# Reordering the first step of a fused Perceiver layer: weight loads, key products, key norms and the threefold query row

## The reference

```python
x = x + cross_attention(layernorm(x), ctx)   # x 1x128x512, ctx 1x12544x512, 16 heads of 32
x = x + self_attention(layernorm(x))         # 16 heads of 128, FP4 codes times scales as weights
x = x + moe(layernorm(x))                    # 32 experts of 256, 4 chosen per row, and a shared one

# cross_attention:
q     = rms_norm(x @ q_w.T + q_b) * norm_q_w
k_img = rms_norm(ctx[:257] @ k_img_w.T + k_img_b) * norm_k_img_w
v_img = ctx[:257] @ v_img_w.T + v_img_b
k, v  = the same of ctx[257:], with k_w, v_w, ... of their own
out   = (attention(q, k_img, v_img) + attention(q, k, v)) @ o_w.T + o_b
```

## Time and profile before

| | us |
|---|---|
| median of three executions | 1211.16 |
| lowest, highest | 1208.44, 1211.66 |
| span of the profiled execution | 1210.0 |
| TensorE, VectorE, ScalarE, GpSimd busy | 1172.7, 979.3, 853.0, 763.8 |

### The profile page before, as it was taken

One profiled execution on the slowest core, in us unless ns is written; L12 is line 12 of the kernel. 1 busy time (PEld: TensorE's weight loads), 2 busy tenths in 40 slices (PEclk: granted clock), 3 DMA queues, 4 the chain that ended last, 5 costly groups with the idle time before them and its releaser, 6 DMA issues.

```text
span 1210.0 us, 26425 instructions
## 1 busy us (share of the span) xinstructions
PE 1172.7 (97%) x8794; PEld 940.5 (78%) x8794; DVE 979.3 (81%) x1657; ACT 853.0 (70%) x1845; POOL 763.8 (63%) x1064
## 2 busy tenths in 40 slices
PE   6999999999999999999999999999999779899998
PEld 4768888888888888888888888888887558588886
DVE  4768888878888888888888887888877779499997
ACT  5567777777767777777777777677777757378885
POOL 7987888888888878788887888888873100000000
PEclk9999999999999999999999999999999989999999
DMA  7135686665776667756668666686653899469990
GB/s 253 41 97 154 164 218 168 172 171 151 212 177 176 166 168 186 207 155 175 171 168 215 168 175 163 154 218 171 175 135 97 257 394 397 190 253 366 360 365 21
DMA packets 132400, 236.74 MB, mean 196 GB/s; under 512 B 18086, under 2 KB 45222, under 8 KB 131884
## 3 DMA queue, kind: packets, MB, share of 16 engines
q1 hardware_dynamic: 132268, 235.06, 66.4%
HBM read 140.87 MB, written 17.04 MB: 130 GB/s over the span
## 4 chain that ended last, share of the span: by engine, by line
PE 89%; POOL 5%; DVE 2%; issue 1%; ACT 1%; DMA 1%; SPq 0%; POOLq 0%; DVEq 0%; ACTq 0%
PE ps L1500 36%; PE ps L1363 18%; PE ps L1526 9%; PE ps L1570 8%; PE ps L1694 3%; PE ps L1697 3%; PE ps L1700 3%; PE ps L1715 1%; PE ps L1723 1%; PE ps L1719 1%; PE ps L1671 1%; PE ps L1610 1%; PE ps L1614 1%; PE ps L1607 1%; POOL cx_blocks L613 1%
## 5 line engine op out<-in xcount | busy, mean ns | idle before, releaser
L1500 PE MATMUL ps<-w_text,cx_blocks 128*128 128x512 f32 x1974 | 536.7, 397 | 1.3 <-ACT v_first L803 0.7
L1500 PEld LDWEIGHTS ps<-w_text,cx_blocks 128*128 128x128 f32 x1974 | 366.4, 189 | 65.8 <-issue 2.7
L846 ACT ACTIVATE p<-ps,small 128x512 f32<-128x512 f32 (+2 forms) x400 | 271.1, 678 | 203.1 <-DVE small L1167 199.7
L1165 DVE TENSOR_REDUCE small<-ps 128x1 f32<-128x512 f32 (+2 forms) x400 | 270.6, 677 | 110.2 <-PE ps L1526 109.9
L1363 PE MATMUL ps<-ident,p 128*128 128x128 f32 x1584 | 239.8, 273 | 8.8 <-DVE pt L1158 7.0
L1363 PEld LDWEIGHTS ps<-ident,p 128*128 128x128 f32 x1584 | 193.9, 140 | 63.9 <-issue 12.4
L1526 PE MATMUL ps<-k_stack,q_stack 96*128 96x512 f32 (+1 forms) x400 | 191.9, 480 | 1.2 <-ACT p L846 1.2
L828 ACT ACTIVATE pt<-ps 128x512 f32<-128x512 f32 (+1 forms) x250 | 147.6, 591 | 12.3 <-PE ps L1363 8.0
L615 POOL TENSOR_TENSOR cx_blocks<-cx_sum,cx_blocks 128x256 fp32r<-128x256 f32 x188 | 139.3, 741 | 14.8
L613 POOL TENSOR_TENSOR cx_blocks<-cx_sum,small 128x256 fp32r<-128x256 f32 x188 | 118.2, 629 | 44.8 <-PE ps L1500 37.0
L1167 DVE TENSOR_TENSOR small<-small 128x1 f32<-128x1 f32 x400 | 132.4, 331 | 13.7
(11 more groups left out here) (252 smaller groups left out, 1935.2 us busy)
## 6 DMA issues: line engine op xcount, KB each, us to landing
expert<-experts SPq DMA_DIRECT2D x34, 1536.0 KB, 8.7
k_stack<-kt_hi SPq DMA_DIRECT2D x384, 128.0 KB, 2.5
cx<-ctx_t SPq DMA_DIRECT2D x48, 512.0 KB, 4.4
k_stack<-kt_lo SPq DMA_DIRECT2D x192, 128.0 KB, 2.5
codes<-codes SPq DMA_DIRECT2D x64, 256.0 KB, 4.5
code_scale<-code_scales SPq DMA_DIRECT2D x256, 64.0 KB, 4.0
scaled<-codes SPq DMA_DIRECT2D x64, 256.0 KB, 4.4
weight_q<-scaled SPq DMA_DIRECT2D x1, 4096.0 KB, 15.6
```

The lines of the kernel that those rows point to most:

```text
L846: eng.activation(pb[:, lo:hi], score_bank(s, h)[:, lo:hi], exp, bias=nm[1 - par][:, h:h + 1], accum_out=ls[1 - par][:, h:h + 1]).then_inc( ...
L1165: eng.tensor_reduce(ngm[:, h:h + 1], score_bank(s, h)[:, lo:hi], AX.X, ALU.max, negate=True).then_inc(e_gm, 1)
L1500: last = eng.matmul(ps_a[(p + i + 1) % 2][:, :], blk[:, i, a, c * P:(c + 1) * P], w_t[:, i, w, c * D:(c + 1) * D], start=(i in FRESH and c ...
```

## The change

It touches the first step alone:

- SyncE issues the image key weights ahead of the two further context tiles and of wq.
- TensorE does `product(0, 0)` and `product(0, 1)` ahead of the query's product and the last three spread rows.
- VectorE stores the first two key tiles ahead of the query; the image value split comes behind the query's bias. The threefold repeat leaves VectorE: it makes a plain 128x512 product into `q_sq`, and ScalarE repeats it into `q_thrice`, as it did before for the text part's query.
- GpSimd has the norms of key tiles 0 and 1 ahead of the query's norm; between that and `first_pair`'s low part nothing is left.
- ScalarE squares two key tiles ahead of the query, squares the third ahead of storing the first transposes, and then repeats the query.

```diff
@@ sync
             eng.dma_start(img_cx[:, :, 0:P], cxt[:, :, 0:P]).then_inc(e_cx0, 16)
+            load_weight(0)
             eng.dma_start(img_cx[:, :, P:IT * P], cxt[:, :, P:IT * P]).then_inc(e_cx, 16)
             eng.dma_start(wq[:, :, :], wview(t["q_wt"])).then_inc(e_wq, 16)
-            load_weight(0)
             load_weight(1)
@@ gpsimd, image()
                 eng.tensor_tensor(pair_hi[:, :, :], keys, ones.broadcast_to((P, DC, 2 * P)), ALU.mult).then_inc(e_ahi, 1)
+                key_norm(0, 0, 1)
+                key_norm(0, 1, 1)
                 eng.wait_ge(e_qsq, 1)
                 eng.tensor_scalar(r_t, q_ss, RMS_EPS, float(HD), ALU.add, ALU.mult).then_inc(e_pool, 1)
                 n_pool[0] += 1
                 eng.wait_ge(e_pool, n_pool[0])
                 eng.tensor_tensor(q_r, r_t, minus_half, ALU.pow).then_inc(e_rs, 1)
 
-                key_norm(0, 0, 1)
                 eng.wait_ge(e_ahi, 1)
                 eng.tensor_tensor(pair_lo[:, :, :], keys, pair_hi[:, :, :].bitcast(F32), ALU.subtract).then_inc(e_ab, NPOS)
                 eng.wait_ge(e_w[2], 16)
                 eng.wait_ge(e_w[3], 16)
                 eng.tensor_tensor(t1[:, :, :], b12, b11, ALU.subtract).then_inc(e_tt, 1)
-                key_norm(0, 1, 1)
@@ scalar
+            def repeat_queries(i, of):
+
+                eng.wait_ge(e_qh, i + 1)
+                eng.activation(q_thrice[i][:, :, :].rearrange("p h (r d) -> p h r d", r=NST),
+                               of[:, :].rearrange("p (h d) -> p h d", h=NH).unsqueeze(2).broadcast_to((P, NH, NST, HD)),
+                               copy).then_inc(e_q3, 1)
...
                 split_weight(1)
+                square_keys(0, *IMAGE_TILES[0])
+                eng.wait_ge(e_sq, 1)
+                square_keys(0, *IMAGE_TILES[1])
                 eng.wait_ge(e_qb, 1)
                 eng.activation(q_sq[:, :], qf[:, :], square, scale=D ** -0.5, accum_out=q_ss).then_inc(e_qsq, 1)
-                square_keys(0, *IMAGE_TILES[0])
                 for i in range(3, NROW):
                     store_row(i)
                 scale_keys(0, *IMAGE_TILES[0])
                 split_weight(2)
-                square_keys(0, *IMAGE_TILES[1])
-                keys_high(0, *IMAGE_TILES[0])
                 eng.wait_ge(e_sq, 2)
                 square_keys(0, *IMAGE_TILES[2])
+                keys_high(0, *IMAGE_TILES[0])
+                repeat_queries(0, q_sq)
@@ vector, image()
-                eng.wait_ge(e_rowc, 1)
+                eng.wait_ge(e_rowc, 2)
+                keys(0)
+                keys(1)
                 eng.wait_ge(e_qp, 1)
                 eng.tensor_tensor(qf[:, :], ps_s[0][:, :], q_rows[:, 0, :], ALU.add).then_inc(e_qb, 1)
-                eng.wait_ge(e_rowc, 2)
-                keys(0)
                 split_weight(1)
                 eng.wait_ge(e_rowc, NROW)
                 eng.wait_ge(e_rs, 2)
                 chain(eng.scalar_tensor_tensor(qn[:, :], qf[:, :], q_r, q_rows[:, 1, :], ALU.mult, ALU.mult))
-                keys(1)
-                eng.tensor_tensor(q_thrice[0][:, :, :].rearrange("p h (r d) -> p h r d", r=NST), by_stack(qn[:, :]),
-                                  by_stack(q_rows[:, 2, :]), ALU.mult).then_inc(e_qh, 1)
+                eng.tensor_tensor(q_sq[:, :], qn[:, :], q_rows[:, 2, :], ALU.mult).then_inc(e_qh, 1)
@@ tensor
-            eng.wait_ge(e_lnxc, 1)
-            eng.wait_ge(e_wq, 16)
-            for c in range(DC):
-                last = eng.matmul(ps_s[0][:, :], ln_xt[:, c * P:(c + 1) * P], wq[:, c, :], start=(c == 0), stop=(c == DC - 1))
-            last.then_inc(e_qp, 1)
-            for i in range(3, NROW):
-                spread_row(i)
+            def project_queries():   # the lines above, as a function
...
                 for j in range(IT):
                     if j < 2:
                         eng.wait_ge(e_rowc, j + 1)
+                    else:
+                        project_queries()
                     product(0, j)
```

More of the change, by code:

```diff
@@ L785, in image @@
                 stack_queries(0, 0, DC)
-                eng.wait_ge(e_qh, 2)
-                eng.activation(q_thrice[1][:, :, :].rearrange("p h (r d) -> p h r d", r=NST),
-                               qf[:, :].rearrange("p (h d) -> p h d", h=NH).unsqueeze(2).broadcast_to((P, NH, NST, HD)),
-                               copy).then_inc(e_q3, 1)
+                repeat_queries(1, qf)
                 keys_high(0, *IMAGE_TILES[2])
@@ L1031, in _ @@
             split_weight(0)
-            def by_stack(x):
-                return x.rearrange("p (h d) -> p h d", h=NH).unsqueeze(2).broadcast_to((P, NH, NST, HD))
             def queries_low(i, lo, hi):
@@ L1386, in _ @@
             spread_row(2)
-            eng.wait_ge(e_lnxc, 1)
-            eng.wait_ge(e_wq, 16)
-            for c in range(DC):
-                last = eng.matmul(ps_s[0][:, :], ln_xt[:, c * P:(c + 1) * P], wq[:, c, :], start=(c == 0), stop=(c == DC - 1))
-            last.then_inc(e_qp, 1)
-            for i in range(3, NROW):
-                spread_row(i)
+            def project_queries():
+                eng.wait_ge(e_lnxc, 1)
+                eng.wait_ge(e_wq, 16)
+                for c in range(DC):
+                    last = eng.matmul(ps_s[0][:, :], ln_xt[:, c * P:(c + 1) * P], wq[:, c, :], start=(c == 0), stop=(c == DC - 1))
+                last.then_inc(e_qp, 1)
+                for i in range(3, NROW):
+                    spread_row(i)
             def transpose_queries(i):
-                eng.wait_ge(e_q3 if i else e_qh, 1)
+                eng.wait_ge(e_q3, i + 1)
                 if i > 0:
```

## The result

| | before | after |
|---|---|---|
| median of 11 executions each, us | 1211.66 | 1217.61 |
| lowest, highest | 1206.22, 1213.0 | 1213.62, 1220.35 |
| span of the profiled execution | 1210.0 | 1214.5 |
| ratio after to before, 95% interval | | 1.0049 [1.0031, 1.0067] |

The interval lies wholly above 1.003, the 0.3% that the prediction took as the least that can be told from no change: the changed kernel is slower. The predicted time was 1216.5 us, the forecast slower.

The account below looks back on a forecast made before the run. TensorE, busy 97%, was taken as the bound, waiting early on a chain over GpSimd. The middle of +4.2 and +7.1 less 0.28, taken as +5.3, gave span 1215.3, time 1216.5 us; own range 1214.3 to 1218.8, all cases down to 1208.5.

Parts of the forecast that it names:

- The start: First weight split: ScalarE from 10.75, VectorE's part to 15.0 us; up to 1 us more from GpSimd, none taken.
- The rival reading: First key products: TensorE at the high clock from 15.0, query done at 23.9, 2.9 us earlier; no chance given.
- The query chain: From the query's bias to the third key tile: value product starts at 37.4 instead of 30.30, 7.1 us later.
- Two handovers: Query chain: q_normed waits for first_pair, q_sq for w_sum; chance 0.62, 0.59 of it above +3.6 us.
- The rivals with one handover or none: Query chain: q_sq directly behind q_normed, +3.1 us, 1214.3, chance 0.14; or no wait, no change, 1211.2, chance 0.12.
- The 7.65 us from the first value product to the second: TensorE, 30.30 to 37.95 before: the product again starts at the low clock, so this length stays.
- second value product: Sum at TensorE's place at 37.95 us: between +4.2 and +7.1 us later; +5.3 taken with the wait of 0.28.
- The wait of 0.28 at 48.92 goes: TensorE behind the value products: its one wait of 0.28 us there disappears.
- both schedules arrive some 5 us late: TensorE's and GpSimd's runs behind the first 50 us: some 5 us late, nothing behind gives it back.
- One of the stated signs: GpSimd's later w_sum: 4 to 5 us later than 35 if the prediction is right.
- Key norms ahead: GpSimd's queue: two pairs at 22 to 26 us free; one pair less later, worth about 0.8, up to 2.8 us.
- Threefold row by ScalarE: Query repeat: 3.74 us off VectorE, 1.52 hidden on ScalarE; gain eaten by waits before q_normed and q_sq.

Follow-up runs that it names:

- e1: Changed kernel with GpSimd's first_pair low and first w_sum moved ahead of the query's norm; 1215.42 us, ratio to before 1.0030.
- b2: The kernel of b1 with three added float32 matmuls on TensorE while it waits for the first split; 1211.29 us, ratio to before 0.9984.
- e3: Changed kernel with three added float32 matmuls keeping TensorE busy ahead of the key products, output unchanged; 1215.96 us, ratio to before 1.0031.
- b1: The kernel of e1 with GpSimd's first plain key tile norm earlier and second w_sum ahead of the third key norm; 1211.75 us, ratio to before 0.9994.
- e2: Changed kernel with only GpSimd's first w_sum moved behind the third key norm; 1216.20 us, one execution.
- e4: Kernel before with only the threefold query repeat moved from VectorE to ScalarE; 1212.01 us, ratio to before 0.9998.
- b3: Kernel before's order of loads and products, with ScalarE's repeat and GpSimd's queue rearranged, ScalarE's second weight split later; 1210.62 us, ratio to before 0.9995.
- e6: Changed kernel with the loads in the old order (context tiles, wq, then image key weights); 1223.75 us, one execution.

## Why the prediction was right, step by step

*The start.* ScalarE's split was put at 10.75 and came at 10.65; VectorE's end at 15.0 and came at 14.88; TensorE began at 14.94. The 1 us that GpSimd might take at VectorE's start was not taken in this trace: GpSimd's `img_cx_lo` (11.46 to 12.73) was all but done when VectorE's split was issued at 12.58, and the split took 2.30; GpSimd's next `img_cx_hi` (1.04 elsewhere) took 3.09 behind it. In e1, b2 and e3 the context landed later, `img_cx_lo` ran to 13.48, 13.35 and 13.71, and the split took 3.04, 2.91 and 3.28. So up to 1 us there hangs on when the context lands, and that it was put at nothing came true by luck.

*The clock at the start.* The rival reading, that TensorE has the high clock at 15.0 because the column shows 1.00, was wrong; e3 shows the difference, 0.80 against 0.50 for the same matmul. The low clock lasted to about 20.0, 5.1 us, where 5.9 were taken from the earlier trace rows. In b1 it lasted some 3.4 us from the start at 15.56, so the 5.9 was no safe number. The query's product came at 22.96, put at 23.3, and ended at 26.55, put at 26.8.

*The query chain.* Split end 29.9 predicted, 29.48 measured; norm 30.6, 30.17; `q_normed` 33.7, 33.06; `q_sq` 36.6, 35.81; tile stored 37.3, 36.59; value product 37.4, 36.73. Two handovers, in the predicted order, and both nearly of the predicted length (from the norm to the end of `q_normed` 2.9 us where 3.1 were taken, from there to the end of `q_sq` 2.75 where 2.9 were taken). Of the 0.7 us that the whole is early, 0.4 are there at the split's end, from the clock's earlier rise, and the rest comes from the handovers. The rivals with one handover or none are out: the end of `w_sum` lies between `q_normed` and `q_sq`.

*The clock at the value product.* The 7.65 us from the first value product to the second were said to stay; they became 6.75. The windows of after (columns as above) show the low level during the stop and the rise:

```profile
33.00:34.00 1.00, 0.00 (x0) 0.00 (x0) 0.97 (x2) 0.00 (x0) 1.00 (x1) 0.91 0.44 65
34.00:40.00 6.00, 3.27 (x8) 2.62 (x9) 4.55 (x4) 3.30 (x6) 3.55 (x4) 0.50 0.23 77
40.00:41.00 1.00, 1.00 (x5) 0.79 (x4) 1.00 (x1) 0.51 (x1) 0.81 (x1) 0.68 0.06 16
```

0.68 in the last is a rise at about 40.6, 3.9 us after the product began, where before it was 5.9. So the term "second value product" was bounded at +4.2 and +7.1, taken at 5.3 with the wait, and measured +5.5.

That the forecast came so near has luck in it. The mechanism as argued, two handovers and a product that starts low and takes its 7.65 us, gives the upper bound, +7.1. The 5.3 is the middle between it and a bound with the high clock from 15.0 us on, against which the prediction itself had held the pace of the query's matmuls. The one ground for a value near the middle was GpSimd's run at +5.2, and its `first_pair` began 4.8 later (30.13, before 25.38). What brought 7.1 down to 5.5 was an arrival 0.7 earlier and a clock that rose 3.9 instead of 5.9 us after the start, worth 0.9, and neither was foreseen. The sum also has slips that change nothing: 5.65 less 0.28 is 5.37, not 5.3, and the upper end of the range with all that it names comes to 1219.0, not 1218.8.

*What follows.* "The wait of 0.28 at 48.92 goes" was wrong: it is there at 54.54 with 0.36, because VectorE's text split was stretched to 4.41 and GpSimd came as late as TensorE did. That both schedules arrive some 5 us late and nothing gives it back was right: 5.6 at 54.54, 5.6 at 68.03, 5.7 at the marker. The spans of the two profiled executions are only 4.5 apart, the medians of eleven 5.95. 1211.66 + 5.7 is 1217.4, measured 1217.61. The predicted 1216.5 was low by 0.5 in the median that it started from (1211.16, of three executions) and by 0.4 in this term. One of the stated signs was off: GpSimd's second `w_sum` was to come 4 to 5 us later and began 3.2 later (38.43, before 35.24); the third sum, held behind VectorE's text split, is then 5.3 later (43.04, before 37.74).

*Key norms ahead.* "Worth about 0.8 us later" was nothing: GpSimd stands idle for 2.31 us ahead of its third key norm, waiting for the key tile, so an instruction less in front of it wins nothing. "Free" was right.

*Threefold row by ScalarE.* That the gain is eaten by the wait in front of `q_normed` and `q_sq` is what e2 and e1 against the changed kernel show; e4 adds that even in the old order it is below what can be told.

The cause is shown by b1: with every part of the change in place, and only three long instructions and one pair of small ones moved in GpSimd's queue, the loss is gone. That the long ones are what stretched `q_normed` and `q_sq` is shown by e1 and e2 row by row. What b1 does not tell apart is how much of the time at the marker is VectorE's holding and how much is GpSimd's own earlier run: the moves also fill GpSimd's idle time (19.25 to 22.00 us in the changed kernel), and e2, which frees `q_sq` and leaves GpSimd's run as late as it was, gave nothing at the marker. Nor do the moves free VectorE wholly: the value split is 2.85 in b1 and 3.08 in b2. What these moves alone would do to the kernel before was not run; b3 comes near to it and shows no gain.

What the change could win, an earlier start of the key products, did not reach the end: the query came 10 us later, TensorE still stops for 1.7 us at the value product in b1, and without the earlier loads (e6) all is 3.8 us worse, some 0.9 of it by that trace's later landing.

## What to carry to other kernels

Where a trace shows two engines taking turns, as VectorE and GpSimd do here, count a short instruction on the critical path together with the long one of the other engine that may stand in front of it, anew at every dependence inside the chain: two instructions of 0.7 us in a row cost 5.5. Put the other engine's long instructions, by queue order or by a wait of their own, where this engine reads PSUM or stands idle, and do it for both schedules: here a gain on one alone came back as a wait a few products on. A hole in the bound engine's timeline is not yet a gain: closing 2.2 us of one of 3.2 (b3) moved the median by 0.8, within the noise.

## What the runs showed of the hardware

The exclusion holds for a GpSimd instruction over a single column too: the first of the query's norm takes 1.41 us in the changed kernel and 1.98 in e1 (0.20 for a single-column instruction at 34.54 in b1), and each ends 0.05 us behind VectorE's split; the 2.69 us in b1's rows (0.55 elsewhere) end 0.4 behind it.

By the spacing of its matmuls (0.43 and 0.23 us), TensorE went to the high clock 5.1, 3.9 and 5.9 us after it began again (changed kernel at 14.94 and 36.73, before at 30.30), and some 3.4 us after in b1 (at 15.56), so the delay is not one number. A stop of 1.71 us (e1) or 2.17 (e4) left the clock high, one of 3.23 (before) or 5.19 (changed kernel) did not. And the column for the granted clock can't be trusted at the start: it shows 1.00 in 18:19 of the changed kernel, where the matmuls come 0.43 apart.
